# A graph layer on one core: another order of plain and paired edge tiles, regions used twice, and loads issued from another engine

## The reference

```python
h = jnp.maximum(_layernorm(x, axis=-1), 0.0)
row, col = src, dst                       # edge_index = stack([src, dst])
msg = jnp.concatenate([h[col], edge_attr], axis=1)
m = jax.nn.relu(msg @ W1a.T + b1a)        # 128 wide, per edge
m = m @ W1b.T + b1b
sums = segment_sum(m, row, n_nodes); counts = segment_sum(ones, row, n_nodes)
agg = sums / jnp.maximum(counts, 1.0)[:, None]
z = jax.nn.relu(jnp.concatenate([h, agg], axis=1) @ W2a.T + b2a)
z = z @ W2b.T + b2b
out = jnp.concatenate([z, h], axis=1) @ Wr.T + br
return x + out
```

## Time and profile before

| what | us |
|---|---|
| median of the runs | 528.64 |
| the profiled execution | 527.18 |
| its span, first to last instruction | 525.4 |
| PE, DVE, ACT, POOL busy | 410.0, 338.0, 234.7, 348.6 |
| mean granted clock of PE | 0.905 of full |

### The profile page before, as it was taken

The page is one execution under the profiler, slowest core; times in us unless marked ns, Lnnn a source line. Parts: engine busy times, 40 slices in busy tenths (PEclk is TensorE's granted clock), DMA queues, the critical chain, the costliest instruction groups (busy, mean ns, idle before and its releaser), DMA issues.

```text
span 525.4 us, 8550 instructions
## 1 busy us (share of the span) xinstructions
PE 410.0 (78%) x2889; PEld 364.1 (69%) x2889; DVE 338.0 (64%) x786; ACT 234.7 (45%) x540; POOL 348.6 (66%) x404
## 2 busy tenths in 40 slices
PE   5644655999789898687789888997887889986791
PEld 4434545875678787676678778897776878985681
DVE  7778364455485876738376776877635766767781
ACT  3331815441565266476716346373463354400370
POOL 4777777766277777777777777776772777777000
PEclk9776977795879999888999999999789999999996
DMA  7996998522499599776879689699249999787511
GB/s 187 317 326 159 261 255 272 163 94 75 146 307 297 206 333 275 211 247 208 317 230 307 209 249 366 227 343 276 102 146 372 293 339 308 242 272 215 138 44 43
DMA packets 66077, 123.19 MB, mean 234 GB/s; under 512 B 8793, under 2 KB 35726, under 8 KB 66030
## 3 DMA queue, kind: packets, MB, share of 16 engines
q1 hardware_dynamic: 53518, 90.80, 57.4%
q0 software_dynamic: 12512, 31.80, 17.9%
HBM read 67.86 MB, written 54.70 MB: 233 GB/s over the span
## 4 chain that ended last, share of the span: by engine, by line
PE 36%; DVE 23%; POOL 13%; issue 9%; DMA 8%; ACT 5%; SPq 4%; DVEq 0%; ACTq 0%; POOLq 0%
POOL slots_dram L632 12%; PE bank L1392 8%; PE bank L1374 7%; PE bank L1402 7%; DMA dstb<-in_dst 5%; PE bank L1356 5%; DVE perm L810 5%; DVE oh L859 3%; PE bank L1327 2%; PE bank L1427 2%; DVE sums L885 2%; DVE x_hi L798 2%; DVE x_lo L800 2%; PE bank L1424 1%; DMA rows<-slots_dram 1%
## 5 line engine op out<-in xcount | busy, mean ns | idle before, releaser
L632 POOL DMA_INDIRECT slots_dram<-pay,pos_i x271 | 265.2, 978 | 99.0 <-issue 80.2
L1392 PE MATMUL bank<-rows,oh 128*125 128x130 f32 x1150 | 141.0, 279 | 26.3 <-DVE oh L859 25.9
L1392 PEld LDWEIGHTS bank<-rows,oh 128*125 128x125 f32 x1150 | 133.1, 190 | 33.7 <-issue 32.5
L859 DVE TENSOR_TENSOR oh<-bank,rows 128x1500 f32<-128x1500 f32 (+5 forms) x72 | 85.7, 1194 | 33.1 <-DMA rows<-slots_dram 20.0
L618 POOL DMA_INDIRECT pairs_dram<-pay,pos_c x80 | 76.9, 962 | 37.2 <-issue 21.6
L1131 ACT ACTIVATE pay<-bank 128x512 f32<-128x512 f32 x68 | 39.5, 594 | 95.8 <-PE bank L1356 95.6
L1356 PE MATMUL bank<-pw,eo 128*128 128x128 f32 x542 | 73.4, 292 | 3.8 <-ACT pay L1131 2.6
L1356 PEld LDWEIGHTS bank<-pw,eo 128*128 128x128 f32 x542 | 69.2, 206 | 5.0 <-ACT pay L1131 3.0
L1144 ACT ACTIVATE eo<-dstb,minus_lane 64x512 f32<-64x512 int32 x56 | 39.8, 711 | 72.1 <-DMA dstb<-in_dst 54.9
L1402 PE MATMUL bank<-perm,x_hi 116*128 116x256 f32 (+1 forms) x160 | 42.3, 354 | 25.3 <-DVE perm L810 25.2
L1374 PE MATMUL bank<-pwx,moved 128*128 128x131 f32 x320 | 47.2, 306 | 10.3 <-ACT pw L1120 7.8
(11 more groups left out here) (215 smaller groups left out, 485.9 us busy)
## 6 DMA issues: line engine op xcount, KB each, us to landing
rows<-slots_dram SPq DMA_DIRECT2D x16, 864.0 KB, 7.9
rows<-pairs_dram SPq DMA_DIRECT2D x16, 864.0 KB, 11.6
dstb<-in_dst SPq DMA_DIRECT2D x34, 256.0 KB, 9.1
eo<-in_edges_T SPq DMA_DIRECT2D x34, 256.0 KB, 8.6
slots_dram<-zeros SPq DMA_DIRECT2D x9, 756.0 KB, 10.5
pairs_dram<-zeros SPq DMA_DIRECT2D x6, 864.0 KB, 18.9
rows<-slots_dram SPq DMA_DIRECT2D x8, 648.0 KB, 9.5
xs<-in_edges_rows SPq DMA_DIRECT2D x20, 232.0 KB
```

The source lines that it names most:

```text
L632: pool.indirect_dma_start(out=slots_dram[:, :], out_offset=bass.IndirectOffsetOnAxis(ap=pos_i[:, u, k:k + 1], axis=0), in_=pay[:, u, k, :] ...
L859: V.tensor_tensor(oh2[:, r % 2, 0:n, :], marks_near.unsqueeze(1).to_broadcast((128, n, BN)), rows[:, sum_no[r] % RR, 0:n, MARK:ONE].to_bro ...
L1392: last = T.matmul(o[0:BN, v * SW:(v + 1) * SW], oh2[:, r % 2, n, :], rows[:, sum_no[r] % RR, n, 0:SW], start=(t == 0), stop=(t == TB[ph] - ...
```

## The change

- `ORDER` becomes `"OOOO" + "CO" * 3 + "CCO" * 2 + "CO" * 4 + "OOOO"`: 28 pairs, 11 of them C; twice two C pairs follow each other (groups 20 to 23 and 26 to 29). The last O pair holds the remaining 29 edges, one tile. Phases are `[5, 5, 3, 2, 2]`, C regions `[5, 5, 1]`, the last with one tile by two for each bucket. There are 25 x 24 = 600 sum tiles, of which 291 and the tail's 25 come after group 46 or later; before, these are 250 and 25 of 575.
- Regions of phases 2, 3 and 4 lie over those of 0 and 1, without a clear: their marks get 128 added, the comparison takes 128 off, and old rows then match no node. POOL waits, before the first scatter of such a phase, until the old region has been loaded.
- `ready` lets node rounds start at group 14 and only in O groups.
- From n = 6 the edge loads, and from n = 10 the `dst` loads, are issued by ACT in `onehot`.
- Both groups' `features` and ACT's `round_features` of a C pair come ahead of the pair; in `rounds_after` the first stands between a round's one-hot and the taking of the round before.
- At the end each engine waits for the flag's value (`bd`) instead of the last output, and SP waits for the output after its test.

```diff
-ORDER = "OOOO" + "CO" * 10 + "OOO"
+ORDER = "OOOO" + "CO" * 3 + "CCO" * 2 + "CO" * 4 + "OOOO"
...
-    PAIRS = [5, 5, 3, 2, 1, 1]
-    PAIRED = [5, 5]
+    PAIRS = [5, 5, 3, 2, 2]
+    PAIRED = [5, 5, 1]
...
+    OVER = [None, None, 0, 1, 1]
+    FRESH = [ph for ph in range(NPH) if OVER[ph] is None]
...
+    TAG = [0 if ph in FRESH else 128 for ph in range(NPH)]
...
-    AFTER_PHASE = [4, 4, 2, 1, 1, 0, 4, 2]
+    AFTER_PHASE = [4, 4, 2, 1, 0, 4, 2, 2]
...
+    NODES_FROM = 14
...
-        return kind != "sum" or g >= END_GROUP[ph] + AFTER_PHASE[ph]
+        if kind != "sum":
+            return g >= NODES_FROM and g in O_GROUPS
+        return g >= END_GROUP[ph] + AFTER_PHASE[ph]
...
-                if g >= 6 and g in C_GROUPS:
-                    load_paired_edges(C_GROUPS.index(g))
-                elif g >= 6:
+                if g >= 6 and g in O_GROUPS and n < ACT_FROM + DB:
                     load_dst(n)
-                    load_edges(n)
                     n += 1
-                for ph in range(1, NPH):
+                for ph in FRESH[1:]:
...
+                for c in paired_next(g if g in C_GROUPS else g + 1):
+                    load_paired_edges(c)
...
-                    pool.wait_ge(s_fill[STARTS.index(n // 2)], 16 * len(CLEAR_PIECES))
+                    ph = STARTS.index(n // 2)
+                    if ph in FRESH:
+                        pool.wait_ge(s_fill[ph], 16 * len(CLEAR_PIECES))
+                    else:
+                        for r in range(RR):
+                            pool.wait_ge(s_rows[r], loads_of(OVER[ph], r))
...
-                if half == 0:
-                    features(c)
...
+                if ph < NPH and TAG[ph]:
+                    V.scalar_tensor_tensor(oh2[:, r % 2, 0:n, :], seen, -float(TAG[ph]), near, ALU.add, ALU.is_equal).then_inc(S["oh2"], 1)
...
             def rounds_after(g):
+                ahead = paired_next(g)
+                ranked = any(rounds[r][0] == "crank" for r in after[g])
...
                     hots(r)
+                    if ahead and not ranked and g not in C_GROUPS:
+                        features(ahead.pop(0))
                     if r >= 1:
                         take(r - 1)
...
+                for c in ahead:
+                    features(c)
...
             def onehot(n):
                 g = O_GROUPS[n]
+                act.wait_ge(S["H"], made(O_GROUPS[n - EB]))
+                act.dma_start(eo[rest_half(n), n % EB, :], edges_T[:, g * GE:(g + 1) * GE]).then_inc(s_ea_in[n % EB], 16)
                 act.wait_ge(s_dst[n % DB], 16 * (n // DB + 1))
-                act.wait_ge(S["H"], made(O_GROUPS[n - EB]))
...
+                if n + DB < len(O_GROUPS):
+                    g = O_GROUPS[n + DB]
+                    act.dma_start(dstb[p, n % DB // 2, :], dst[g * GE:(g + 1) * GE].rearrange("(o e) -> o e", o=1).to_broadcast((WS, GE))
+                                  ).then_inc(s_dst[n % DB], 16)
...
-            sp.wait_ge(S["out"], 16 * sum(len(parts) for parts in OUT_PARTS))
-            sp.wait_ge(S["flag"], 1)
+            sp.wait_ge(S["bd"], 1)
             is_bad = sp.value_load(flag[0:1, 0:1], min_val=0, max_val=1)
...
+            sp.wait_ge(S["out"], 16 * sum(len(parts) for parts in OUT_PARTS))
```

More of the change, by code:

```diff
@@ L354, in gnn_layer @@
         s_dst = [sem(f"dst_loaded_{u}") for u in range(DB)]
-        s_fill = [sem(f"regions_cleared_{ph}") for ph in range(NPH)]
+        s_fill = {ph: sem(f"regions_cleared_{ph}") for ph in FRESH}
         s_sc = [sem(f"rows_scattered_{u}") for u in range(PB)]
@@ L372, in region, with loads_of @@
             return slots_dram[first:first + m * C[ph] * 128, :].rearrange("(v p t) w -> p v (t w)", p=128, t=C[ph])
+        def loads_of(ph, u):
+            return 16 * max([0] + [n // RR + 1 for n, r in round_of.items() if rounds[r][1] == ph and n % RR == u])
         def round_tiles(r):
@@ L384, in gnn_layer, with paired_next @@
         unit_round = {n: r for r, n in perm_no.items()}
+        def paired_next(g):
+            return [C_GROUPS.index(g + v) for v in (1, 2)] if g % 2 and g + 1 in C_GROUPS else []
         def made(g):
@@ L696, in _, with phase_of @@
             link(V.scalar_tensor_tensor(srcq[:], srci[:], -float(NB), src_in[:], ALU.mult, ALU.add))
+            def phase_of(j):
+                return sum(j >= first for first in STARTS[1:])
             def ranks_a(j):
@@ L1222, in _ @@
                     late_weights()
-                if g in O_GROUPS and g + 1 in C_GROUPS:
-                    round_features(C_GROUPS.index(g + 1))
+                if g + 1 == C_GROUPS[0]:
+                    for c in paired_next(g):
+                        round_features(c)
                 if g + EB in O_GROUPS and O_GROUPS.index(g + EB) >= ACT_FROM:
```

51 lines of the change are left out of this document (33 added, 18 removed).

## The result

| what | before | changed |
|---|---|---|
| median of the runs, us | 528.64 | 555.89 (552.58 to 557.99, four runs) |
| the profiled execution, its span | 527.18, 525.4 | 557.26, 555.5 |
| PE's mean granted clock | 0.905 | 0.874 |
| POOL's waits for ACT's results | 33.5 | 72.2 |

The change makes the kernel slower: 1.0489 times the time before (1.0406 to 1.0572), 26 us. The prediction had 521.8 us and a range of 507 to 537. Medians of the kernel before ran from 528.7 to 532.2 us from one batch to the next, so all that follows goes by ratios within a batch. The changed kernel was timed in one batch only; to compare it with an edited one is to compare two ratios, each with its own interval.

What follows compares the result with a forecast made beforehand. The prediction took a chain through DVE, PE, ACT and back to DVE as the bound, with POOL following. Its terms summed to -6.8 us: 520.4 us under the profiler, 521.8 as median, range 507 to 537.

Steps and rivals of the forecast that it cites:

- Step 1: Ahead of group 46, one C pair more and one O pair fewer: +12.7 us (+8 to +15).
- Step 2: Six scatters fewer on POOL: -7.6 us there, 0 in the sum because it lies beside the chain.
- Rival A: Whole kernel: the chain gives way and POOL becomes the bound; -38 us, 490.6 us; chance 0.07.
- Step 3: Sum tiles, 600 for 575, with 16 leaving the middle and 41 coming after group 46: +7 us.
- rival C: Last stage cannot take 41 more tiles; row buffers' landing sets the pace: +16 us, 537.8 us; chance 0.25.
- Step 4: Node rounds (h, z) move from groups 7 to 12 to 14, 15, 18 and 25: -9 us (0 to -17.3).
- Step 5: Late groups' dst and edge loads go from SP to ACT: -3 early, -3 and -8 from DVE's row waits.
- Step 6: ACT issues 27 edge and 23 dst loads, partly ahead of a copy PE waits for: +4 us (0 to +31).
- Step 7: Both groups' features come before a C pair's first permutation: -4 us (+5 to -17).
- Step 8: Region reuse, with added tag and POOL's new waits at groups 38 and 48: 0.
- Step 9: Tail and closing: -1.1 us for last rows, -2.4 (-1 to -3) for reading the flag before the output lands.

Runs made afterwards that it cites:

- nodes_early: The changed kernel with node rounds allowed from group 7 on, as before the change; 1.0413 of the kernel before.
- shares_cc_6: The changed kernel with 6 instead of 2 tiles of sum rounds allowed per step from C to C group; 1.0346 of the kernel before.
- ranks_in_o: The changed kernel with the rank pass of each row's second C pair one group earlier, in the O group ahead; 1.0532 of the kernel before.
- pool_late: The kernel before with four small unread iotas on POOL ahead of the scatters of each of the O groups 46 to 53; 1.0253 of the kernel before.
- pool_mid: The kernel before with four small unread iotas on POOL in each of the eight O groups 30 to 43; 1.014 of the kernel before.
- eleven_alternating: The changed kernel with 28 pairs, 11 of them C, but no two C pairs in a row; 1.0072 of the kernel before.
- closing_only: The kernel before with the new closing alone: engines read the flag once counts are checked, only SP waits for the output; 0.9885 of the kernel before.

## Why the prediction was wrong

Its sum was -6.8 us; measured is +26. By the ladder of ratios, times 528.6: new code in the old order -9.5, the eleventh C pair +13.3, the rows of C pairs +22.0. My steps 1 to 3 had +19.7 for the eleventh pair and its tiles, steps 4 to 9 had -26.5 for the code, and nothing in the sum stood for the rows. So of the miss of some 33 us the rows are 22, the gains that did not come 17, and 6 go the other way. Without the rows, at 1.0072, the time would have been 532.4 and inside the range.

- **Step 1** is the one that failed. +12.7 was right for an extra C pair (+13.3 with its tiles and fewer scatters, steps 1 to 3 together, for which I had +19.7). But it priced the pair as if it stood alone. I wrote that no row shows two C pairs in a row, bounded the step between groups, and left the price of the neighbourhood at nothing. The forecast "18 us after the one before" came out at 19.4 and 20.3 us for the second pair of a row, 1 to 2 us long. The first pair of each row took 24.8 and 28.7, where the other C pairs from group 30 on take 17.5 to 23.3, with the next pair's ranks (group 20, 26) among its permutations and the sums and z rounds of group 25 ahead of them; nodes_early and shares_cc_6 take 7.6 and 5.3 us of the second, and moving the ranks (ranks_in_o) won nothing. In the CO order an O pair is also the cover for the 8 us of ACT and DVE steps that lie bare between groups 21 and 22.
- **The reading of POOL** was wrong for the kernel before. I took the 33.5 us of the earlier trace rows to show that POOL only follows, and wrote that nearly nothing waits for it. But the chain that ended last runs over POOL's scatters and the issue gaps between them from 416.60 to 484.79, and SP waited for them too (engine, line, what was waited for: us in total, times, longest):

```profile
SPq L504 <- DMA slots_dram<-pay,pos_i: 23.6, 2, 21.6
```

  pool_late and pool_mid show that it leads there. This is not what made the changed kernel slow: there POOL's new waits show where the groups came late, and the end waited for the left-over sum rounds, 13.7 us behind the last scatter. Step 2's zero holds: eleven_alternating has its last scatter at 478.4, 6.4 us earlier than the kernel before, and gains nothing by it. Rival A named POOL as a bound, but of the changed kernel and as a total, not stage by stage.
- **Step 3 and rival C.** The last stage, from group 46 ready to the tail, is 12.0 us longer with 41 tiles more. Step 3 had +7 for all tiles, which is some +11 there and -4 in the middle, so it was near. PE was busy for 87.6 of the 97.3 us. This stage was longer through its sum rounds, as rival C had it. C's condition was met for the rows from `slots_dram` (median landing 13.4 us, above its 8.8), but its consequence did not come: DVE's waits for rows fell from 29.1 to 9.1 us. So C's sign was right and a part of its cost, but its mechanism, rounds paced by the landing of their rows, is not what happened, and the larger part of the loss lies ahead of group 46.
- **Step 4** (-9): nothing. On the chain z and h rounds of groups 14 to 18 and 25 show 21.6 us against 17.3, with a granted clock of 0.58 at 142 to 167; group 15 comes 16.1 us after 14 where it was 3.3. Putting them back changes -0.8% in the new order and nothing that can be told in the old one.
- **Step 5** (-3, -3, -8): ACT's wait for `dst` fell from 54.9 to 18.1, and DVE's waits for rows by 20 us, yet the time did not follow. No run has the loads on ACT alone. In the old order steps 4 to 8 together, for which I had -23, make the 0.7% or 3 us that the closing leaves. What I missed is that SP, freed of edge loads, was given both loads of a C pair at once, ahead of all else. It stands there 209 us (longest 33.9), where it was 78.7 before, and moving them back took 1.0%. The Trainium skill, "DMA: Bandwidth & Descriptors", section "Rules for kernel authors", has it that spreading loads over engines saves the issuing engine's time alone. The 3 us of the old order fit its zero better than my -8, but steps 4, 6 and 7 are in them too, and by the two intervals they are uncertain by some 5 us either way, so this is not shown.
- **Step 6** (+4): ACT's DMA issues take 0.47 us each (so the timeline has them), and ACT is 5% of the chain. PE's wait for ACT's window copy is at most 2.6 as before, not the 3.7 that I gave as a sign.
- **Step 7** (-4): no gain in the old order (0.982 and 0.976) and a loss of some 9 us in the new one (1.0489 against 1.0314, with the paired loads). Features of both groups ahead put ACT's rounding behind the relu of the C group before.
- **Step 8** (0): not tested apart; POOL's only wait for a region's loads that the trace shows is 0.3 us.
- **Step 9** (-2.4): right in kind and too small: closing_only has 6 us. That the difference is the flag's way through DVE and the other engines was not tested apart.

What I gave as signs would have shown it: groups 12 to 15 were to be ready 10 to 15 us earlier. 12, 13 and 14 were 3, 8 and 8 us earlier, and 15 was 5 us later. The last sign, that something waits for POOL, was there as well: in the changed kernel SP waits 27.6 us for its scatters (longest 15.7).

## What to carry to other kernels

Price a step by its neighbours: when two steps of a kind come to stand side by side, list what each engine does between them and what hid it before. Ask of an engine with a backlog not only who waits for it, but at which points its backlog is spent (a region's closing, the last stage). And before naming it as what sets the end of a changed kernel, look at what the last stage's first instruction waited for: here it was POOL's rows before, and PE's and DVE's own rounds after, although POOL's waits had more than doubled. Test code and order apart: here one hid a gain of 1.8% behind a loss of 5%.

## What the runs showed of the hardware

- The same permutation matmuls start 0.24 us per two with a granted clock of 1.00 and 0.43 with 0.50. The fall came within one group of the changed kernel: 1.00 at 213.0 to 214.2 and 0.50 at 214.6 to 216.5, after PE had stood idle for 2.39 us and then for 0.40. Dummy matmuls in the gap behind that group brought the full level back for the next (1.00 at 226.6 to 229.0), at a cost that ate the gain.
- A DMA issue takes 0.47 us on ACT (median, edge and `dst` loads alike), against 0.60 and 0.66 on SP.
- Four small iotas on POOL between indirect DMAs, 1.25 us busy, widen the gap from 0.31 to 1.43 us: they use the small issue gap too, so that 1.1 us a time is what they cost.
